# A four-layer graph network on one core: the attention's weighted sums formed with the exponentials as stationary operand

## The chip, the cores and the metric

The kernel runs on one core of a Trainium2 chip. The metric is the device time of one execution in microseconds. An execution is compared by the median of several runs; one execution was also recorded by the hardware profiler.

## What is computed

A graph of 625 nodes (768 features each) and 10,000 edges passes through four residual blocks, each behind a layer norm and a ReLU. The first two blocks are relational convolutions, the last two are attention over the edges. Cut to what matters here, an attention block does, for each head with its features `h` (8 heads of 96 in one layer, then one head of 768, and in the last block 12 heads of 64):

```
e = leaky_relu(al_s[src] + al_d[dst], 0.2)
m = segment_max(e, dst)
ex = exp(e - m[dst])
z = segment_sum(ex, dst)
out = segment_sum(h[src] * (ex / z[dst])[:, :, None], dst)
```

## The kernel before

The kernel is written engine by engine, with semaphores between them; the order of the work on each engine is the order of its program. The attention is computed densely. The edges stand as a matrix of counts between source and destination nodes, 640 x 640 with padding (`NG` = 5 tiles of `P` = 128 source nodes, `NP` = 640 destination nodes along the free axis), and its logarithm is added to the scores, so that an exponential carries the number of edges with it and is zero where there are none. What the texts below call n=0 is the layer with eight heads (`C2` = 96), n=1 the one with one head, n=2 the one with twelve (`C3` = 64). `tiles_` exists on PE and on ScalarE (ACT in the profile), `all_heads` on VectorE (DVE).

A step is one head and one tile of source nodes; there are 5 x 8 = 40 of them in n=0 and 5 x 12 = 60 in n=2, numbered k. For step k, four things happen:

- TensorE (PE) forms the *terms* in PSUM (`log_terms`, L2049): the logarithms of the counts, in a high and a low fp32r part, and the maxima per destination, as three products in two halves of 320 columns. The terms alternate between banks 0, 1 and 4, 5.
- ScalarE forms `z`, the leaky score (L829); VectorE adds the terms to it (`logits`, L1496).
- ScalarE takes the exponential into one of two buffers `pt` (L837), an array of 128 source nodes by 640 destination nodes in fp32.
- PE sums over the source nodes (L2084). Stationary is `R`, the node features of this head with a column of ones (c + 1 = 97 or 65 columns), moving is `pt`, 640 columns in two halves, in banks 2 and 3. After five steps there stand c + 1 rows of sums over 640 nodes.

PE's program is two steps ahead: the terms of k + 2 come before the sums of k. After a head's five steps, its sums stand with features along the partitions, while the output wants nodes there. So ScalarE copies them to `oT` (`sums_copy`, L845), PE transposes them in five pieces into bank 6 (`turned`, L2072), and VectorE divides by the column of ones and adds the result in (`head_out`, L1506, with L1559 for n=0 and `residual`, L1647 to L1651, for n=2). PE waits for the copy at the next head's first sums, since the banks are the same ones, and does the transposes right behind these.

VectorE also computes the next pair of heads' maxima (`maximum`, L1471), whose columns PE turns into rows (`head_rows`, L2036) and ScalarE copies (L818). In VectorE's program `head_out` of a head stands behind the fourth logits of the next one. In the last pair of heads no maximum is left. In n=0 a long pass of VectorE over the first half of the output (`elu_parts(0)`, L1549 to L1552) stands ahead of the last head's output.

A fp32 matmul appears in the trace as two records, each with its own load of the stationary operand (PEld); a transpose or a fp32r or fp16 matmul as one.

Of the kernel before, what the change touches and what calls it, by code (L numbers as in the profile page):

```python
# [21 lines left out]
P = 128  # L22
N, D, E = 625, 768, 10000
NG = -(-N // P)
NP = NG * P
# [29 lines left out]
def gnn_kernel(nc, a, out):  # L55
    ctx = ExitStack()
    with ctx:
# [19 lines left out]
        R = sb("R", [P, NG, 780])  # L77
# [5 lines left out]
        arena = sb("arena", [P, 6528 + GB * D])  # L83
# [6 lines left out]
        zt = arena[:, 2560:5760].rearrange("p (b n) -> p b n", b=NG)  # L90
        pt = arena[:, 5760:7040].rearrange("p (b n) -> p b n", b=2)
        alT = arena[0:2 * H3, 7680:8320]
        oT = arena[:, 7680:8320]
        rowD = arena[:, 8320:9600].rearrange("p (b n) -> p b n", b=2)
        mx_scr = [arena[:, o:o + NP] for o in (7040, 9600, 10240)]

# [84 lines left out]
        with nc.sbuf_tensor("sc_lo", [P, SCW], F32R) as sc_lo:  # L181
# [17 lines left out]
        ident = sb("ident", [P, P])  # L199
        iota = sb("iota", [P, P + 2])  # L200
        iota16 = sb("iota16", [P, NP + 1], F16)
        z16 = sb("z16", [P, 512], F16)
# [22 lines left out]
        ps = ctx.enter_context(nc.psum_tensor("ps", [P, 8, 512], F32))  # L225
# [25 lines left out]


        A = [{m: sem(f"{m}_{n}") for m in ("al_ok row_tp row_cp row_st rs0 rd0 mx mx_ok cl_ok c_ok z_ok l_ok p_ok o_mm o_ev"
                                           + (" rs1 rd1 o_cp o_tp o_r" if n != 1 else "")).split()} for n in range(3)]

        FT_BANK = (4, 0)
        HEADS = ((H2, C2), (1, D), (H3, C3))
# [343 lines left out]
        def _(act):  # L601
            cp, rl = ACT.Copy, ACT.Relu
# [217 lines left out]
            def tiles_(n, out_tile):  # L820
                H, s = HEADS[n][0], A[n]

                def z(it, i):

                    j, t = i // NG, i % NG
                    if t == 0:
                        act.wait_ge(s[f"rd{j % 2}"], 16 * (it + j // 2) + 16)
                    act.wait_ge(s["p_ok"], 10 * it + i + 6)
                    act.activation(zt[:, t, :], rowD[:, j % 2, :], rl,  # L829
                                   bias=AL[n][:, t, 3, ds(2 * it + j, 1)], scale=0.8).then_inc(s["z_ok"], 1)  # L830

                def e(it, i):

                    act.wait_ge(s["l_ok"], 10 * it + i + 1)
                    if H > 1:
                        act.wait_ge(s["o_mm"], 10 * it + i + 1)
                    act.activation(out_tile(i % 2, i % NG), zt[:, i % NG, :], ACT.Exp,  # L837
                                   bias=AL[n][:, i % NG, 2, ds(2 * it + i // NG, 1)]).then_inc(s["p_ok"], 1)

                def sums_copy(hd):  # L840

                    c = HEADS[n][1]
                    act.wait_ge(s["o_mm"], 5 * hd + 7)
                    act.wait_ge(s["o_tp"], hd + 1)
                    act.activation(oT[0:c + 1, :].rearrange("p (b n) -> p b n", b=2), ps[0:c + 1, 2:4, 0:NP // 2], cp).then_inc(s["o_cp"], 1)  # L845

                def heads(it, m, last):

                    for i in range(m):
                        if not (last and i + 3 >= m):  # L850
                            z(it, i + 3)
                        e(it, i)
                        first = isinstance(it, int) and it == 0
                        if H > 1 and i % NG == 0 and not (first and i == 0):
                            sums_copy(2 * it + i // NG - 1)
                        if i % NG == 4 and not last:
                            head_rows(n, it + 1, i // NG, 0)
                        if H > 1 and i == 2 and not first:
                            head_rows(n, it, 1, 1)
                        if i == NG + 2 and not last:  # L860
                            head_rows(n, it + 1, 0, 1)
                for i in range(3):
                    z(0, i)
                if H == 1:
                    heads(0, NG, True)
                else:
                    heads(0, 2 * NG, False)
                    with act.Fori(1, H // 2 - 1) as it:
                        heads(it, 2 * NG, False)
                    heads(H // 2 - 1, 2 * NG, True)  # L870
                    sums_copy(H - 1)

            act.wait_ge(S["ct_ln"], 1)
            logs(0)
# [6 lines left out]
            for k in range(2):  # L881
                act.wait_ge(S["elu_m"], k + 1)
                c = slice(k * HALF, (k + 1) * HALF)
# [35 lines left out]
        def _(dve):  # L919
# [466 lines left out]
            for k in range(2):  # L1386
                for g in range(NG):
# [7 lines left out]
                    else:  # L1395
                        ins = dve.tensor_tensor(x[:, g, :], x[:, g, :], vec[:, 1, :], ALU.add)
# [4 lines left out]
            for i in range(2 * NG):  # L1401
                c, j = i // NG, i % NG
# [95 lines left out]
            def head_out(n, it, j, put, steps):  # L1498

                H, c = HEADS[n]  # L1500
                s = A[n]
                hd = 2 * it + j
                base = steps * hd
                o = ps[:, 6, 0:NG * (c + 1)].rearrange("p (g c) -> p g c", c=c + 1)
                dve.wait_ge(s["o_tp"], hd + 2)
                dve.tensor_scalar(rz[:, j, :].unsqueeze(2), o[:, :, c:c + 1], 1e-16, None, ALU.add if n == 0 else ALU.max).then_inc(s["o_r"], 1)  # L1506
                dve.wait_ge(s["o_r"], base + 1)
                dve.reciprocal(rz[:, j, :], rz[:, j, :]).then_inc(s["o_r"], 1)
                dve.wait_ge(s["o_r"], base + 2)
                put(hd, o[:, :, 0:c], rz[:, j, :].unsqueeze(2).to_broadcast([P, NG, c]), s, base)  # L1510
# [64 lines left out]
            first = n_chain[0]  # L1575
            for i in range(4 * NG):
                c, g, k = i // (2 * NG), i // 2 % NG, i % 2
# [13 lines left out]
            for k, slope in ((2, 0.2), (3, 0.8)):  # L1591
                ins = dve.tensor_scalar(AL[1][:, :, k, :], AL[1][:, :, 0, :], slope, None, ALU.mult)
# [23 lines left out]
            for g in range(NG):  # L1616
                b = 4 + 2 * (g % 2)
# [6 lines left out]
                for k in range(2):  # L1624
                    cols = slice(k * HALF, (k + 1) * HALF)
                    ins = dve.scalar_tensor_tensor(x[:, g, cols], ps[:, b + k, 0:HALF], rz[:, 0, g:g + 1], x[:, g, cols], ALU.mult, ALU.add)
# [11 lines left out]
            for k, slope in ((2, 0.2), (3, 0.8)):  # L1638
                ins = dve.tensor_scalar(AL[2][:, :, k, :], AL[2][:, :, 0, :], slope, None, ALU.mult)
# [18 lines left out]
        def _(pe):  # L1658
# [340 lines left out]
            for i in range(2 * NG):  # L1999
                c, j = i // NG, i % NG  # L2000
# [4 lines left out]
                n = 0  # L2005
                for s in range(NG):
                    if i == 0:
                        pe.wait_ge(S["ct_lo"], s + 1)
                    for l, r in ((cg_hi, rg_hi), (cg_hi, rg_lo), (cg_lo, rg_hi)):
                        ins = pe.matmul(ps[:, 2 + i % GA, 0:HALF], l[:, s, P * j:P * (j + 1)], r[:, s, c * HALF:(c + 1) * HALF],  # L2010
                                        start=(n == 0), stop=(n == 3 * NG - 1))
# [47 lines left out]
            def tiles_(n):  # L2059

                H, c = HEADS[n]
                s = A[n]
                for m, v in (("o_mm", 2), ("o_tp", 1), ("o_ev", 2)):
                    pe.sem_inc(s[m], v)
                first_terms(n)

                def turned(hd):

                    pe.wait_ge(s["o_cp"], hd + 1)
                    pe.wait_ge(s["o_ev"], hd + 2)  # L2070
                    for g in range(NG):
                        ins = pe.transpose(ps[:, 6, (c + 1) * g:(c + 1) * (g + 1)], oT[0:c + 1, P * g:P * (g + 1)], ident[0:c + 1, 0:c + 1])  # L2072
                    ins.then_inc(s["o_tp"], 1)

                for hd in range(H):
                    for t in range(NG):
                        k = NG * hd + t
                        if k + 2 < NG * H:
                            log_terms(n, (k + 2) // (2 * NG), (k + 2) % (2 * NG))
                        if t == 0 and hd:  # L2080
                            pe.wait_ge(s["o_cp"], hd)
                        pe.wait_ge(s["p_ok"], k + 11)
                        for b in range(2):
                            ins = pe.matmul(ps[0:c + 1, 2 + b, 0:NP // 2], R[:, t, (c + 1) * hd:(c + 1) * (hd + 1)],  # L2084
                                            pt[:, k % 2, NP // 2 * b:NP // 2 * (b + 1)], start=(t == 0), stop=(t == NG - 1), skip_group_check=True)
                        ins.then_inc(s["o_mm"], 1)
                        if t == 0 and hd:
                            turned(hd - 1)
                        if t == 1 and hd and hd + 1 < H:
                            head_rows(n, hd + 1, 1)  # L2090
                        if t == 2 and hd + 2 < H:
                            head_rows(n, hd + 2, 0)
                turned(H - 1)

            for n in range(3):
                pe.sem_inc(A[n]["p_ok"], 10)
# [12 lines left out]
            for k, bank in ((0, 6), (1, 2)):  # L2109
                for b in range(2):  # L2110
                    ins = pe.matmul(ps[:, bank + b, 0:CW], ident[0:2, k:k + 1].to_broadcast([2, P]), alT[0:2, CW * b:CW * (b + 1)],
                                    start=True, stop=True)
# [7 lines left out]
            for g in range(NG):  # L2120
                b = 4 + 2 * (g % 2)
                if g >= 2:
                    pe.wait_ge(A[1]["o_ev"], g - 1)
                for k, (c0, c1) in enumerate(((0, HALF), (HALF, D + 1))):
                    for t in range(NG):
                        ins = pe.matmul(ps[:, b + k, 0:c1 - c0], h[:, t, P * g:P * (g + 1)], R[:, t, c0:c1],  # L2126
                                        start=(t == 0), stop=(t == NG - 1))
# [26 lines left out]
            for g in range(NG):  # L2154
# [5 lines left out]
                for kt in range(KT):  # L2160
                    o = 512 * FT_BANK[g % 2] + 2 * P * kt
# [28 lines left out]
```

## Time and profile before

| | before |
|---|---|
| median of 3 runs | 2178.45 us |
| lowest, highest | 2177.02, 2182.46 us |
| profiled execution | 2181.19 us, of which the span 2179.4 |
| PE busy | 1939.9 us (89%) |
| PE weight loads busy | 1699.0 us (78%) |
| DVE busy | 1211.6 us (56%) |
| ACT busy | 838.8 us (38%) |
| L2084, PE, the sums | 400 records, 125.1 us |
| mean granted clock of PE | 0.954 |

The profile is of one execution. The span is what the engines' records cover; the execution's own time is 1.8 us longer. Busy time counts overlapping records once, but a matmul's record includes the time in which it drains while the next one already streams, so a busy PE need not be at its peak. The chain of waits follows the work that ended last back through whatever released it. A weight load (PEld) can run beside a matmul.

### The profile page before, as it was taken

How to read it: one execution, taken by the hardware profiler on the slowest of the kernel's cores; microseconds unless marked ns; L12 is line 12 of the kernel's file. 1: busy time of each engine (PE TensorE's matmuls, PEld its weight loads, DVE VectorE, ACT ScalarE, POOL GpSimd, SP SyncE). 2: the span in 40 equal slices, each digit the busy share in tenths (PEclk: the TensorE clock that was granted, in tenths of full speed). 3: DMA queues.
4: the chain of work that ended last, by engine and by line, in shares of the span. 5: the costliest groups of instructions: out<-in, count | busy, mean ns of one | idle time of the engine just before them, and what ended most of it. 6: DMA issues, size and time to landing. Idle time of an engine off the chain costs nothing.

```text
span 2179.4 us, 34673 instructions
## 1 busy us (share of the span) xinstructions
PE 1939.9 (89%) x11166; PEld 1699.0 (78%) x11167; DVE 1211.6 (56%) x2275; ACT 838.8 (38%) x1125; POOL 559.0 (26%) x538
## 2 busy tenths in 40 slices
PE   5998998989999999779999999996788869878898
PEld 5887986759999977579999999996446857675676
DVE  7842223454443645565555655554555687756696
ACT  2221222332222223224555555553333128631676
POOL 0003765630000056434333444100772000000000
PEclk9999999999999999989999999998899989989999
DMA  5445667754556567657788887875883012100211
GB/s 163 151 154 167 178 170 259 267 163 127 168 168 196 172 232 246 197 175 236 263 274 267 276 265 253 285 236 184 266 271 126 8 37 61 66 15 8 68 61 54
DMA packets 203766, 377.74 MB, mean 173 GB/s; under 512 B 18937, under 2 KB 174378, under 8 KB 203670
## 3 DMA queue, kind: packets, MB, share of 16 engines
q1 hardware_dynamic: 171014, 245.57, 34.9%
q0 software_dynamic: 31216, 128.89, 18.7%
q10 hardware_dynamic: 1440, 1.97, 0.2%
q8 instruction: 65, 1.06, 0.2%
q14 instruction: 31, 0.25, 0.0%
HBM read 288.03 MB, written 88.33 MB: 173 GB/s over the span
## 4 chain that ended last, share of the span: by engine, by line
PE 38%; DVE 6%; issue 5%; DMA 4%; ACT 3%; another core or an unknown queue 1%; POOL 1%; ACTq 0%; SPq 0%; DVEq 0%; POOLq 0%
PE ps L1867 20%; PE ps L2084 4%; PE ps L2049 3%; DMA arena<-in_L_gnn_W_rel 3%; PE ps L1749 2%; PE ps L1896 2%; PE ps L2126 1%; PE ps L1744 1%; PE ps L2010 1%; PE ps L1669 1%; DMA arena<-U,ix 1%; DVE arena L1471 1%; POOL arena L529 1%; PE ps L2036 1%
## 5 line engine op out<-in xcount | busy, mean ns | idle before, releaser
L1867 PE MATMUL ps<-w_hi,hT_hi 128*128 128x384 f32 x2052 | 719.5, 351 | 45.8 <-ACT arena L615 13.8
L1867 PE MATMUL ps<-w_hi,hT_lo 128*128 128x384 f32 x2052 | 695.0, 339 | 0.3 <-issue 0.3
L1867 PE MATMUL ps<-w_lo,hT_hi 128*128 128x384 f32 x2052 | 694.9, 339 | 0.0
L1867 PEld LDWEIGHTS ps<-w_hi,hT_hi 128*128 128x128 f32 x2052 | 391.8, 191 | 55.8 <-issue 19.3
L1867 PEld LDWEIGHTS ps<-w_lo,hT_hi 128*128 128x128 f32 x2052 | 391.5, 191 | 0.4 <-issue 0.2
L529 POOL DMA_INDIRECT arena<-U,ix x252 | 272.1, 1080 | 465.4 <-DMA U<-arena 348.6
L1867 PEld LDWEIGHTS ps<-w_hi,hT_lo 128*128 128x128 f32 x2052 | 391.3, 191 | 0.0
L615 ACT ACTIVATE arena<-ps 128x384 f32<-128x384 f32 x160 | 78.2, 492 | 448.4 <-PE ps L1867 386.4
L1749 PE MATMUL ps<-arena,onehot 128*128 128x512 f32 x504 | 197.6, 516 | 20.1 <-DVE onehot_r L1087 7.5
L1749 PEld LDWEIGHTS ps<-arena,onehot 128*128 128x128 f32 x504 | 91.0, 199 | 99.9 <-issue 95.8
L565 POOL DMA_INDIRECT h<-h_d,lidx x68 | 91.5, 1346 | 295.6 <-PE ps L1896 252.0
L961 DVE TENSOR_TENSOR w_lo<-arena,w_hi 128x2304 fp32r<-128x2304 f32 x45 | 114.9, 2554 | 84.6 <-ACT w_hi L608 76.5
L738 ACT ACTIVATE msg<-arena,wgt 128x768 fp32r<-128x768 f32 x84 | 78.7, 937 | 195.6 <-DMA arena<-U,ix 162.5
L1204 DVE TENSOR_TENSOR w_lo<-arena,w_hi 128x1152 fp32r<-128x1152 f32 x67 | 91.1, 1360 | 86.4 <-ACT w_hi L675 76.7
L685 ACT ACTIVATE arena<-ps 128x384 f32<-128x384 f32 x136 | 66.2, 487 | 177.9 <-PE ps L1867 128.3
L1148 DVE SCALAR_TENSOR_TENSOR hT_lo<-ps,hT_hi 128x512 fp32r<-128x512 f32 x102 | 70.2, 688 | 110.4 <-ACT hT_hi L645 96.9
L2084 PE MATMUL ps<-arena,R 128*65 128x320 f32 (+1 forms) x400 | 125.1, 436 | 2.1 <-ACT arena L837 1.7
L1090 DVE TENSOR_SCALAR onehot<-iota,tab,wgt 128x128 f32<-128x128 f32 x126 | 46.8, 371 | 120.7 <-PE ps L1749 92.0
L1496 DVE TENSOR_TENSOR arena<-arena,ps 128x640 f32<-128x640 f32 x105 | 85.1, 819 | 43.1 <-PE ps L2049 37.2
L1080 DVE SCALAR_TENSOR_TENSOR msg<-arena,wgt,msg 128x768 fp32r<-128x768 f32 x84 | 85.2, 1014 | 40.2 <-issue 24.4
L1031 DVE TENSOR_SCALAR oh_d<-iota,tab 128x128 f16<-128x128 f16 x168 | 44.3, 264 | 100.7 <-PE ps L1711 92.4
L608 ACT ACTIVATE w_hi<-arena 128x2304 fp32r<-128x2304 f32 x45 | 95.6, 2125 | 10.1 <-issue 7.2
(289 smaller groups left out, 2920.6 us busy)
## 6 DMA issues: line engine op xcount, KB each, us to landing
arena<-in_L_gnn_W_rel SPq DMA_DIRECT2D x74, 1152.0 KB, 6.2
U<-arena SPq DMA_DIRECT2D x292, 192.0 KB
arena<-in_L_gnn_W SPq DMA_DIRECT2D x36, 1152.0 KB
U<-z SPq DMA_DIRECT2D x28, 864.0 KB
arena<-rows_d SPq DMA_DIRECT2D x40, 320.0 KB, 3.4
arena<-in_L_gnn_root SPq DMA_DIRECT2D x4, 1152.0 KB
arena<-U,ix POOLq DMA_INDIRECT x252
arena<-in_L_gnn_W_root SPq DMA_DIRECT2D x2, 1152.0 KB
```

The costliest lines, as they stand in the source:

```text
L529: pool.indirect_dma_start(out=ring[:, b, :], out_offset=None, in_=U[0:NP * (R0, R0, R1)[phase], :], in_offset=bass.IndirectOffsetOnAxis(ap ...
L565: pool.indirect_dma_start(out=src_rows[:, TC * j + g, :], out_offset=None, in_=h_d, in_offset=bass.IndirectOffsetOnAxis(ap=lidx[:, 2 * TC ...
L608: act.activation(w_hi[:, o % 2], raw[:, o % 2], cp).then_inc(S["w_hi"], 1)
L615: act.activation(dst, ps[:, (o + g) % 2, 0:HALF] if len(dst.shape) == 2 else ps[:, (o + g) % 2, 0:HALF].rearrange("p (h c) -> p h c", h=ds ...
L738: act.activation(parts_of(ph)[0][:, t // TW % MB, :], ring[:, n % RB, :], cp, scale=wgt[:, ph // 2, t:t + 1]).then_inc(S["msg_hi"], 1)
L961: dve.tensor_tensor(w_lo[:, o % 2], raw[:, o % 2], w_hi[:, o % 2].bitcast(F32), ALU.subtract).then_inc(S["w_lo"], 1)
L1080: dve.scalar_tensor_tensor(lo[:, b, :], ring[:, (NT * ph + t) % RB, :], wgt[:, ph // 2, t:t + 1], hi[:, b, :].bitcast(F32), ALU.mult, ALU. ...
L1204: dve.tensor_tensor(w_lo[:, 1 - j, 0:KT // 2], raw[:, 1 - j, 0:KT // 2], w_hi[:, 1 - j, 0:KT // 2].bitcast(F32), ALU.subtract)
L1496: dve.tensor_tensor(z, z, terms(i % 2), ALU.add).then_inc(s["l_ok"], 1)
L1749: ins = pe.matmul(sums(c0, g), onehot[:, b, :], ring[:, n % RB, c0:c1], start=False, stop=True, skip_group_check=True)
L1867: ins = pe.matmul(acc, l, r[:, j, kt, :], start=(n == 0), stop=(n == 3 * KT - 1))
L2084: ins = pe.matmul(ps[0:c + 1, 2 + b, 0:NP // 2], R[:, t, (c + 1) * hd:(c + 1) * (hd + 1)], pt[:, k % 2, NP // 2 * b:NP // 2 * (b + 1)], st ...
```

## The change

The two operands of the sums change places. Stationary is now a piece of the exponentials, 128 source nodes by 128 destination nodes; moving is `R`, with its 97 or 65 columns. Five matmuls per step take the place of two, and the result comes out with the nodes along the partitions, in one bank: five groups of c + 1 columns, 485 or 325 in all. The banks 2 and 3 alternate between heads. Since five groups share a bank, a matmul with zeros opens the bank for each head, and the sums are all added to it. ScalarE's copy, `oT`, PE's transposes and the semaphores of both are gone; VectorE reads the bank of the sums once the last of the head's sums is counted on `o_mm`. PE waits on `o_ev` for the output of the head before last in place of the copy. n=1 is untouched.

```diff
-                def sums_copy(hd):
-
-                    c = HEADS[n][1]
-                    act.wait_ge(s["o_mm"], 5 * hd + 7)
-                    act.wait_ge(s["o_tp"], hd + 1)
-                    act.activation(oT[0:c + 1, :].rearrange("p (b n) -> p b n", b=2), ps[0:c + 1, 2:4, 0:NP // 2], cp).then_inc(s["o_cp"], 1)
...
-                        if H > 1 and i % NG == 0 and not (first and i == 0):
-                            sums_copy(2 * it + i // NG - 1)
...
-                    sums_copy(H - 1)
...
-                o = ps[:, 6, 0:NG * (c + 1)].rearrange("p (g c) -> p g c", c=c + 1)
-                dve.wait_ge(s["o_tp"], hd + 2)
+                o = ps[:, 2 + j, 0:NG * (c + 1)].rearrange("p (g c) -> p g c", c=c + 1)
+                dve.wait_ge(s["o_mm"], NG * hd + NG + 2)
...
-                def turned(hd):
-
-                    pe.wait_ge(s["o_cp"], hd + 1)
-                    pe.wait_ge(s["o_ev"], hd + 2)
-                    for g in range(NG):
-                        ins = pe.transpose(ps[:, 6, (c + 1) * g:(c + 1) * (g + 1)], oT[0:c + 1, P * g:P * (g + 1)], ident[0:c + 1, 0:c + 1])
-                    ins.then_inc(s["o_tp"], 1)
...
-                        if t == 0 and hd:
-                            pe.wait_ge(s["o_cp"], hd)
+                        if t == 0 and hd >= 2:
+                            pe.wait_ge(s["o_ev"], hd + 1)
+                        if t == 0:
+                            pe.matmul(ps[:, 2 + hd % 2, 0:NG * (c + 1)], z16[:, 0:P], z16[:, 0:NG * (c + 1)], start=True, stop=False, skip_group_check=True)
                         pe.wait_ge(s["p_ok"], k + 11)
-                        for b in range(2):
-                            ins = pe.matmul(ps[0:c + 1, 2 + b, 0:NP // 2], R[:, t, (c + 1) * hd:(c + 1) * (hd + 1)],
-                                            pt[:, k % 2, NP // 2 * b:NP // 2 * (b + 1)], start=(t == 0), stop=(t == NG - 1), skip_group_check=True)
+                        for g in range(NG):
+                            ins = pe.matmul(ps[:, 2 + hd % 2, (c + 1) * g:(c + 1) * (g + 1)], pt[:, k % 2, P * g:P * (g + 1)],
+                                            R[:, t, (c + 1) * hd:(c + 1) * (hd + 1)], start=False, stop=(t == NG - 1), skip_group_check=True)
                         ins.then_inc(s["o_mm"], 1)
-                        if t == 0 and hd:
-                            turned(hd - 1)
...
-                turned(H - 1)
```

PE's order around the first step of n=2's last head, before (L2049 the terms, L2084 the sums, L2072 the transposes):

```order
L2049 MATMUL ps<-mrow,ones_r 128x320 x2
L2084 MATMUL ps<-arena,R 65x320 x2
L2072 MATMUL ps<-ident,arena 128x65 x5
L2049 MATMUL ps<-w_hi,ident_r 128x320 x2
L2049 MATMUL ps<-w_lo,ident_r 128x320 x2
```

and the same place in the changed kernel, whose line numbers are lower (L2038 the terms, L2064 the zeroing matmul, L2067 the sums):

```order
L2038 MATMUL ps<-mrow,ones_r 128x320 x2
L2064 MATMUL ps<-z 128x325
L2067 MATMUL ps<-R,arena 128x65 x5
L2038 MATMUL ps<-w_hi,ident_r 128x320 x2
L2038 MATMUL ps<-w_lo,ident_r 128x320 x2
```

The transposes behind the sums are gone, and one matmul of 325 columns stands ahead of them; the terms on both sides stand where they stood.

ScalarE's order at the end of n=2, before (L829 the scores, L837 the exponentials, L845 the copies):

```order
L837 ACTIVATE arena<-arena,al 128x640
L845 ACTIVATE arena<-ps 65x640
L829 ACTIVATE arena<-arena,al 128x640
L837 ACTIVATE arena<-arena,al 128x640 x4
L845 ACTIVATE arena<-ps 65x640
L57 UNCONDITIONAL_BRANCH
```

and in the changed kernel (L828 the scores, L836 the exponentials):

```order
L836 ACTIVATE arena<-arena,al 128x640
L828 ACTIVATE arena<-arena,al 128x640
L836 ACTIVATE arena<-arena,al 128x640 x4
L57 UNCONDITIONAL_BRANCH
```

The copies are gone and the rest closes up; PE and VectorE wait, behind the last exponential, for the last sums alone.

## Rows read from the trace of the kernel before

**Rows 1.** Windows: stretch, its length, each engine's busy time (instructions), PEclk, DMA share, GB/s.

```profile
1806.00:1886.00 80.00, 79.95 (x435) 61.84 (x434) 60.08 (x145) 63.44 (x94) 0.00 (x0) 1.00 0.15 42
...
2065.00:2152.00 87.00, 86.72 (x482) 62.86 (x480) 78.92 (x197) 68.72 (x104) 0.00 (x0) 1.00 0.22 70
```

**Rows 2.** Chain of waits, eight-head layer: start, length, engine, tile, line, instructions.

```profile
1827.72 1.24 PE ps L2084 x4
...
1836.70 1.08 PE ps L2084 x4
...
1837.78 0.88 PE ps L2049 x6
...
1838.66 1.23 PE ps L2084 x4
...
1839.89 0.42 PE ps L2072 x5
...
1842.29 0.11 PE ps L2036
...
1844.35 0.44 PE ps L2036 x4
```

**Rows 3.** Waits of DVE, 1834 to 1845: waiting for, in total, times, longest.

```profile
DVE arena L1496 <- PE ps L2049: 1.1, 1, 1.1
```

**Rows 4.** Timeline of ACT, twelve-head layer: start, length, instruction.

```profile
2075.95 0.68 ACT L845 ACTIVATE arena<-ps 65x640 f32<-65x640 f32 x1
...
2152.56 0.68 ACT L845 ACTIVATE arena<-ps 65x640 f32<-65x640 f32 x1
```

**Rows 5.** Waits of DVE, 2074 to 2085.

```profile
DVE arena L1496 <- DVE x L1651: 0.2, 1, 0.2
```

**Rows 6.** Waits of DVE, 2151 to 2162.

```profile
DVE arena L1496 <- PE ps L2049: 5.4, 5, 1.8
```

**Rows 7.** Chain of waits, twelve-head layer.

```profile
2087.62 1.29 PE ps L2084 x4
2088.92 0.31 PE ps L2072 x5
2089.22 0.93 PE ps L2049 x6
```

**Rows 8.** Timeline of PE's weight loads, fp32, 5 moving columns.

```profile
37.32 0.29 PEld L1781 LDWEIGHTS ps<-R 125*125 125x125 f32 x2 [2.10 <-DVE R L973]
37.53 0.30 PEld L1782 LDWEIGHTS ps<-R 125*128 125x128 f32 x2
37.75 0.19 PEld L1867 LDWEIGHTS ps<-w_hi,hT_hi 128*128 128x128 f32 x1
```

**Rows 9.** Timeline of PE's weight loads, fp32r, 128 and 256 moving columns in turn.

```profile
888.01 0.31 PEld L1724 LDWEIGHTS ps<-w_hi,hT_hi 128*128 128x128 f32 x2
...
890.09 0.19 PEld L1724 LDWEIGHTS ps<-w_hi,hT_hi 128*128 128x128 f32 x1
```

**Rows 10.** Chain and weight loads of the one-head layer's sums, fp32, 384 columns.

```profile
1967.43 32.57 PE ps L2126 x100
...
L2126 PEld LDWEIGHTS ps<-R,h x100: 186/190/190, 1967.4 to 1999.2; 128*128 128x128 f32 x100
```

**Rows 11.** Timeline of PE: eight zeroing matmuls of 512 columns.

```profile
331.84 1.90 PE L1699 MATMUL ps<-z 128*128 128x512 f16 x8 [0.58 <-ACT arena L615]
```

**Rows 12.** Timeline, end of the eight-head layer.

```profile
1890.62 0.64 PE L2072 MATMUL ps<-ident,arena 97*128 97x97 f32 x5 [0.80 <-ACT arena L845]
...
1892.27 0.16 DVE L1506 TENSOR_SCALAR rz<-ps 128x5 f32<-128x5 f32 x1
```

**Rows 13.** Chain of waits, end of the twelve-head layer.

```profile
2172.10 0.71 ACT arena L845
...
2172.85 0.54 PE ps L2072 x5
...
2173.42 0.17 DVE rz L1506
```

More of the change, by code:

```diff
@@ L92, in gnn_kernel @@
         alT = arena[0:2 * H3, 7680:8320]
-        oT = arena[:, 7680:8320]
         rowD = arena[:, 8320:9600].rearrange("p (b n) -> p b n", b=2)
@@ L253, in gnn_kernel @@
         A = [{m: sem(f"{m}_{n}") for m in ("al_ok row_tp row_cp row_st rs0 rd0 mx mx_ok cl_ok c_ok z_ok l_ok p_ok o_mm o_ev"
-                                           + (" rs1 rd1 o_cp o_tp o_r" if n != 1 else "")).split()} for n in range(3)]
+                                           + (" rs1 rd1 o_r" if n != 1 else "")).split()} for n in range(3)]
         FT_BANK = (4, 0)
@@ L2062, in tiles_ @@
                 s = A[n]
-                for m, v in (("o_mm", 2), ("o_tp", 1), ("o_ev", 2)):
-                    pe.sem_inc(s[m], v)
+                for m in ("o_mm", "o_ev"):
+                    pe.sem_inc(s[m], 2)
                 first_terms(n)
-                def turned(hd):
-                    pe.wait_ge(s["o_cp"], hd + 1)
-                    pe.wait_ge(s["o_ev"], hd + 2)
-                    for g in range(NG):
-                        ins = pe.transpose(ps[:, 6, (c + 1) * g:(c + 1) * (g + 1)], oT[0:c + 1, P * g:P * (g + 1)], ident[0:c + 1, 0:c + 1])
-                    ins.then_inc(s["o_tp"], 1)
                 for hd in range(H):
```

## The prediction

> **What bounds the kernel now.** The change touches two of the four layers only, the attention with eight heads (n=0, 1801 to 1893 us) and with twelve (n=2, 2040 to 2175). So I read, in this order: the windows, to see which engine fills these stretches; the chain of waits inside them, to see the steps that follow one another; and VectorE's waits, to see whether it or TensorE sets the pace. In the windows [rows 1] PE is busy nearly all the time in both, at a granted clock of 1.00 (its upper level, 2.4 GHz), but in n=2 VectorE is busy 79 of 87 us too, against 60 of 80 in n=0. Busy shares cannot tell which of two full engines leads. The chain can.
>
> In n=0 the chain is TensorE alone. A step is two groups: four records of L2084, the weighted sums (two fp32 matmuls, two records each), 1.08 us, and six of L2049, the terms, 0.88; together 1.96 [rows 2]. A head is five steps, 9.80, plus 0.16 for the wait on ScalarE's copy (1.24 and 1.23 where 1.08 is usual), 0.42 for the five transposes L2072, 0.11 and 0.44 for the row transposes L2036: 10.93, and the same group does return after 1838.66 - 1827.72 = 10.94. VectorE waits 1.1 us for PE in one such head [rows 3], so **n=0 is bound by TensorE**.
>
> In n=2 a head takes (2152.56 - 2075.95)/7 = 10.94 us [rows 4], and VectorE waits for nobody but itself [rows 5]: its five logits, five maxima and the head's output (three passes over 320 elements instead of one over 480) fill the head. **n=2 is bound by VectorE**, and the 0.21 us that PE loses there before the copied head (1.29 against 1.08) is mostly slack. Only in its last two heads, where no maximum is left to compute, does VectorE wait again, 5.4 us in one [rows 6].
>
> **What goes.** Of n=0: per head 0.16 of wait and 0.42 of transposes, 0.58. The part that counts ends with the last logits; seven heads are copied and turned before it, so 7 x 0.58 = 4.06. The eighth's copy and transposes are over at about 1891.3, but VectorE comes to its output at 1892.27, after the long ELU passes in front of it [rows 12]: no gain. Of n=2: the heads in the middle gain nothing while VectorE leads. In the opening one head is turned before VectorE takes over, 0.13 + 0.31 + 0.05 = 0.49, where 0.31 is the transposes and 0.05 the slower terms behind them (0.93 against 0.88) [rows 7]. In the last two heads 0.57 and 0.48. At the very end copy (0.71) and transposes (0.54) are bare: they lie between the last sum and VectorE, from 2172.08 to 2173.42 [rows 13], 1.3 without one hand-off. ScalarE loses twenty copies of 0.7 us, which nothing else waited for.
>
> **What comes.** A zeroing matmul of 485 or 325 fp16 columns per head. Eight of 512 take 1.90 us [rows 11], 0.24 each, so 0.22 and 0.15. In n=0 seven count (the first hides behind the wait for the first exponentials), 1.54; in n=2 one in the opening and two at the end, 0.45. The new wait on o_ev asks for the output of the head before last. VectorE runs that output before the logits on which PE's term matmuls of the same step already waited, so it costs nothing.
>
> **What is exchanged** decides. Instead of 4 records with 65 or 97 columns to load and 320 to stream, a step has 5 matmuls, 10 records, each with 128 columns to load and 65 or 97 to stream. The streams are short: transposes of 65 and 97 columns followed at 0.31/5 = 0.06 and 0.42/5 = 0.08 us [rows 7, 2]. So what counts is how often 128 fp32 columns can be loaded, L. Three places bear on it. Loads of this very kind behind matmuls of 5 columns follow at (37.75 - 37.32)/4 = 0.108 [rows 8], the lower end. Loads of fp32r, with 128 and 256 columns to stream in turn, follow at (890.09 - 888.01)/18 = 0.116 [rows 9]. And a load can run beside the stream ahead: with 384 fp32 columns a record takes 32.57/100 = 0.326, though its load alone lasts 0.19 [rows 10]. If it did not run beside a short stream, L would be 0.108 + 0.06 or 0.08, that is 0.17 or 0.19, the upper end. I take **0.112**, between the two rows whose streams are short: the type is that of the first, the stream lengths are those of the second. Then the ten take 1.12 where the four took 1.08: +0.04 a step. Over 38 steps of n=0 that is 1.52, over ten in n=2's opening and eight at its end 0.72.
>
> Against this overlap stands a rule. The Trainium skill (TensorE: Matmul & The Clock Gate, the mechanism in Part 3) says that a weight load overlaps a running matmul only when their row groups differ; here all are full height. By that rule the change would end at the upper end of L, the first rival below; for 384 columns the trace disagrees, 0.326 a record where a load after the stream would add 0.108 to it.
>
> **The sum.** n=0: 4.06 - 1.54 - 1.52 = 1.00. n=2: opening 0.49 - 0.15 - 0.40 = -0.06; last two heads 1.05 - 0.30 - 0.32 = 0.43; end 1.3. Together 2.7 us less. In the middle of n=2 PE's head becomes 10.92 - 0.57 + 0.15 + 5 x 0.04 = 10.70, still under VectorE's 10.94. The profiled execution took 2181.19 us; it would take 2178.5. That execution was 2.7 us above the median of 2178.45, so I forecast **2175.7**, 0.12% less. A measurement of this kernel can tell about 0.3%, 6.5 us, from no change: this is no change.
>
> With d = 10 L - 1.08 the gain is 4.94 - 56 d up to d = 0.09, and past it n=2's middle is bound by TensorE too and loses another 8 x (5 d - 0.455). It is zero at L = 0.117, a loss of 6.5 us at L = 0.124, a gain of 6.5 us at 0.105.
>
> **Rivals.** (1) *The short stream does not hide the load.* L = 0.19 in n=0 and 0.17 in n=2 (d = 0.8 and 0.6). n=0 loses 38 x 0.8 - 2.5 = 28, n=2's opening and end 18 x 0.6 - 0.8 = 10, its middle 8 x (3.0 - 0.455) = 20, less 1.3: about 57 us, 2235. For it: the 0.108 of rows 8 would be the same with or without overlap, since 5 columns take no time. Against it: rows 9, where a load beside 128 and 256 columns has no room for both in 0.116, and rows 10. It decides from L = 0.124 on. Chance 0.09. (2) *A smaller overhead*, L = 0.124 to 0.135, say a hand-over between load and stream that only short streams show. At 0.13 the loss is 56 x 0.22 + 8 x 0.645 - 4.9 = 12.5, 2191. For it: nothing in the trace loads ten such operands in a row with 65 or 97 columns. Chance 0.14. (3) *Loads run further ahead*, under the term streams too: a step would be the larger of all loads, 16 x 0.108 = 1.73, and all streams, 0.88 + 0.8. n=0 would gain 0.23 a step until VectorE bounds it, which is 1.1 us a head below today, so about 8; n=2 about 4 with its end: 2166. Against it: the terms' loads have 0.04 us of room each and would have to be kept in several sets, and no row shows more than one ahead. Chance 0.05; with L under 0.105, faster is 0.11. (4) *The clock falls*, because the array streams for less of each step. Streams doubled, a step would take over 1.76 + 1.1 = 2.9 us, and n=0 alone would lose 35. For it: the streams would fill two thirds of a step. Against it: nothing in today's full stretches [rows 1], which show neither. Chance 0.03.
>
> **The numbers.** The forecast (L from 0.105 to 0.124, within 6.5 us) has 0.63, faster 0.11, slower 0.09 + 0.14 + 0.03 = 0.26. The range goes from 2167, just short of rival 3, to rival 2's upper part, 2192; it leaves out rivals 1 and 4.
>
> **What would show it.** L2084's place in the chain: ten records in 1.1 to 1.16 us; over 1.24, I am wrong to the slow side. n=0's heads at 10.9 - 0.15; n=2's still 10.94 with VectorE waiting only for itself, and PE waiting for ScalarE's exponentials. The last output starts 1.3 us sooner behind the last sum. PEclk stays 1.00 in both windows. If n=2's middle heads change at all, my reading of who leads there is wrong.

## The result, and the profile after

The changed kernel takes 2171.03 us in the median of 16 runs (2165.41 to 2178.56), the kernel before 2177.1 in 16 runs beside them (2170.36 to 2185.84). The ratio is 0.9971, with a 95% interval of 0.9957 to 0.9985: a gain of 0.29%, at the edge of what a measurement can tell. Measured again, beside another set of runs of the kernel before, it was 0.9977 (0.9958 to 0.9996). I had forecast 0.12% and called it no change. The experiments further down ran on three chips, where the kernel before took 2161.8, 2159.6 and 2180.5 us in the median, so a whole time is only ever compared with the kernel before beside it; kernels for which no whole time is given ran once, and only their stretches are read.

The span of the profiled execution fell from 2179.4 to 2174.3 us, by 5.1. Not all of that belongs to the change. I cut both traces at the same events of VectorE: the first and the last logits of n=0, the first logits of n=2, and the starts of the outputs (L1506 before, L1495 after) of n=2.

| stretch, us | before | after | gain | forecast |
|---|---|---|---|---|
| n=0, first to last logits | 83.56 | 81.85 | 1.71 | 1.00 |
| n=2, first logits to second output | 28.61 | 28.60 | 0.01 | -0.06 |
| n=2, second to ninth output: seven middle heads | 76.61 | 76.61 | 0.00 | 0 |
| n=2, ninth to eleventh output | 20.44 | 19.61 | 0.83 | 0.43 |
| n=2, eleventh to twelfth output | 6.38 | 5.10 | 1.28 | 1.3 |
| sum of these | | | 3.8 | 2.7 |

The other 1.3 us of the span lie in stretches that the change does not touch (0.8 ahead of n=0's first logits, 0.5 between the two layers). Over the profiles of all kernels of this study the stretch between the two layers varied from 151.6 to 154.9 us, and n=0's first logits came between 1775 and 1811 us. So the stretches are the sharper measure here, and the table above is repeated below for each experiment.

The windows of the changed kernel, over the stretches that answer to [rows 1]:

```profile
1806.00:1883.00 77.00, 77.00 (x623) 75.73 (x622) 58.90 (x142) 58.99 (x85) 0.00 (x0) 1.00 0.18 44
...
2065.00:2149.00 84.00, 83.45 (x668) 80.62 (x666) 76.14 (x191) 63.01 (x93) 0.00 (x0) 1.00 0.21 68
```

The granted clock stayed at 1.00 in both, though TensorE now streams for less of each step. The chain of waits through one head of n=0, beside [rows 2] (L2038 the terms, L2064 the zeroing matmul, L2067 the sums, L2025 the row transposes):

```profile
1826.85 0.22 PE ps L2064
1827.07 1.09 PE ps L2067 x10
1828.15 0.90 PE ps L2038 x6
1829.06 1.09 PE ps L2067 x10
1830.15 0.11 PE ps L2025
1830.26 0.87 PE ps L2038 x6
1831.13 1.09 PE ps L2067 x10
1832.22 0.44 PE ps L2025 x4
1832.65 0.88 PE ps L2038 x6
...
1837.51 0.22 PE ps L2064
```

The four records of 1.08 us have become ten in 1.09; the wait in front of them (1.23 and 1.24) and the 0.42 of transposes are gone; 0.22 for the zeroing matmul has come. Sums and terms together, 1.09 + 0.90, are 1.99 us where they were 1.96. Where row transposes (L2025) stand between the two, the terms take 0.87 or 0.88 and the step costs nothing or 0.01 more than before. A head returns after 1837.51 - 1826.85 = 10.66 us where it was 10.94. The same in n=2, beside [rows 7]:

```profile
2094.40 0.94 PE ps L2038 x6
2095.34 0.15 PE ps L2064
2095.49 1.06 PE ps L2067 x10
2096.55 0.93 PE ps L2038 x6
```

Ten records in 1.06. And the sums' loads and matmuls as the trace groups them (min/median/max ns):

```profile
L2067 PEld LDWEIGHTS ps<-R,arena x1000: 186/192/201, 1805.5 to 2167.9; 128*128 128x128 f32 x167
...
L2067 PE MATMUL ps<-R,arena x1000: 217/275/351, 1805.5 to 2168.0; 128*128 128x65 f32 x100, 128*128 128x97 f32 x67
```

How often one load follows another is read inside a group: seven of its loads, as the timeline shows them in n=0 (97 moving columns) and in n=2 (65).

```profile
1829.12 0.86 PEld L2067 LDWEIGHTS ps<-R,arena 128*128 128x128 f32 x7
...
2152.26 0.86 PEld L2067 LDWEIGHTS ps<-R,arena 128*128 128x128 f32 x7
```

From the first start to the last end are 0.86 us, the last load itself lasts 0.19, so six intervals take 0.67: a load starts every 0.112 us, in both layers. Each lasts 192 ns from start to end, so they overlap with each other's tail and with the streams. The whole group in the chain, 1.09 and 1.06, is a little less than ten such intervals. The first of its loads has run beside the long stream of the last term; and the last of its streams is short, so that the load of the first term behind it ends in the terms' part of the chain (0.90 and 0.93 instead of 0.88). Only the sum of the two, 1.99 in both layers, is a cost.

The outputs of n=2, which cut its stretches (the second, the ninth, the eleventh and the twelfth), beside [rows 4]:

```profile
2067.00 0.16 DVE L1495 TENSOR_SCALAR rz<-ps 128x5 f32<-128x5 f32 x1
...
2143.61 0.16 DVE L1495 TENSOR_SCALAR rz<-ps 128x5 f32<-128x5 f32 x1
...
2163.22 0.16 DVE L1495 TENSOR_SCALAR rz<-ps 128x5 f32<-128x5 f32 x1
...
2168.32 0.16 DVE L1495 TENSOR_SCALAR rz<-ps 128x5 f32<-128x5 f32 x1 [2.28 <-PE ps L2067]
```

From 2067.00 to 2143.61 are seven heads of 10.94 us, as before. The end, beside [rows 13]: the chain goes from the last exponential through the last sums straight to VectorE, with no copy and no transposes between.

```profile
2166.07 0.84 ACT arena L836
...
2166.95 1.34 PE ps L2067 x10
...
2168.32 0.17 DVE rz L1495
```

### The profile page after: what moved, and what is told of

It reads as the page before. It is cut to its first block, busy times and chain, and to the rows that moved or that the text cites. A ratio compares the mean times of both kernels' runs of the same rounds, so it can differ in the third digit from the quotient of the medians.

```text
span 2174.3 us, 35621 instructions
## 1 busy us (share of the span) xinstructions
PE 1936.9 (89%) x11686; PEld 1749.4 (80%) x11687; DVE 1213.3 (56%) x2275; ACT 829.9 (38%) x1105; POOL 553.6 (25%) x538
## 4 chain that ended last, share of the span: by engine, by line
PE 39%; DVE 7%; DMA 4%; issue 4%; ACT 2%; POOL 1%; ACTq 0%; DVEq 0%; another core or an unknown queue 0%; SPq 0%; POOLq 0%
PE ps L1856 22%; PE ps L2067 3%; PE ps L2038 3%; DMA arena<-in_L_gnn_W_rel 2%; PE ps L1885 2%; PE ps L1738 2%; PE ps L2106 1%; PE ps L1999 1%; PE ps L1733 1%; PE ps L1658 1%; DMA arena<-U,ix 1%; POOL arena L528 1%; DVE arena L1460 1%; DVE arena L1485 1%; DVE h L934 0%
## 5 line engine op out<-in xcount | busy, mean ns | idle before, releaser
L1738 PE MATMUL ps<-arena,onehot 128*128 128x512 f32 x504 | 193.1, 506 | 19.8 <-DVE onehot_r L1076 7.6
L2067 PE MATMUL ps<-R,arena 128*128 128x65 f32 (+1 forms) x1000 | 124.1, 271 | 2.1 <-ACT arena L836 2.1
L2067 PEld LDWEIGHTS ps<-R,arena 128*128 128x128 f32 x1000 | 122.6, 191 | 3.4 <-ACT arena L836 2.7
```

What stands on the lines that cost most here:

```text
L1738: ins = pe.matmul(sums(c0, g), onehot[:, b, :], ring[:, n % RB, c0:c1], start=False, stop=True, skip_group_check=True)
L2067: ins = pe.matmul(ps[:, 2 + hd % 2, (c + 1) * g:(c + 1) * (g + 1)], pt[:, k % 2, P * g:P * (g + 1)], R[:, t, (c + 1) * hd:(c + 1) * (hd + ...
```

## The experiments

The stretches of the table above, for each kernel (us; n=0 first to last logits; n=2 as cut above):

| kernel | n=0 | n=2 opening | seven middle | two last | end |
|---|---|---|---|---|---|
| before | 83.56 | 28.61 | 76.61 | 20.44 | 6.38 |
| after | 81.85 | 28.60 | 76.61 | 19.61 | 5.10 |
| e_nozero | 80.46 | 28.65 | 76.61 | 19.29 | 5.10 |
| e_twozero | 83.32 | 28.75 | 76.61 | 19.88 | 5.10 |
| e_moving33 | 81.32 | 28.37 | 76.62 | 19.59 | 5.08 |
| e_load64 | 83.35 | 27.61 | 76.61 | 18.13 | 4.56 |
| e_load96 | 74.24 | 27.67 | 76.57 | 17.90 | 4.83 |
| e_dve_before | 83.60 | 28.60 | 75.68 | 20.42 | 5.97 |
| e_dve_after | 82.09 | 28.59 | 73.85 | 19.72 | 4.69 |
| e_unroll_before | 83.34 | 28.39 | 75.68 | 20.63 | 6.37 |
| e_unroll_after | 81.85 | 28.37 | 73.84 | 19.95 | 5.09 |
| e_best | 80.52 | 28.24 | 72.73 | 19.46 | 5.09 |
| e_after_again | 81.97 | 28.60 | 76.58 | 19.62 | 5.10 |
| e_best_again | 80.26 | 28.23 | 72.73 | 19.45 | 5.10 |

A stretch that an edit does not reach comes back within some 0.3 us, most within 0.1.

### Where TensorE's time counts: the zeroing matmul taken away and doubled

```diff
-                        if t == 0:
-                            pe.matmul(ps[:, 2 + hd % 2, 0:NG * (c + 1)], z16[:, 0:P], z16[:, 0:NG * (c + 1)], start=True, stop=False, skip_group_check=True)
...
-                                            R[:, t, (c + 1) * hd:(c + 1) * (hd + 1)], start=False, stop=(t == NG - 1), skip_group_check=True)
+                                            R[:, t, (c + 1) * hd:(c + 1) * (hd + 1)], start=(t == 0 and g == 0), stop=(t == NG - 1), skip_group_check=True)
```

> The changed kernel without its zeroing matmul: the first matmul of a head in its bank opens it, the four groups behind it only add. My theory (TensorE bounds the eight-head layer, VectorE the middle heads of the twelve-head layer): an eight-head head gets 0.22 us shorter (10.66 to 10.44), seven times, so 1.5 us; the middle heads of the twelve-head layer stay at 10.95; its last two heads give 0.3. Together about 1.9 us less than the changed kernel. The rival (TensorE bounds both layers) expects 0.15 us less in each of the middle heads too, together 3.1 us.

> The changed kernel with the zeroing matmul twice, so 485 or 325 more columns for each head on TensorE. My theory: an eight-head head grows by 0.20 to 0.22 us (10.66 to 10.87), the middle heads of the twelve-head layer stay at 10.95, the last two give 0.3: 1.8 us more. The rival (TensorE bounds the middle heads too) expects them at 11.09.

Taken away: n=0 fell by 1.39 us, its heads from 10.66 to 10.44, the two last heads of n=2 by 0.32, the seven middle ones by nothing. Measured whole, 0.9959 of the kernel before (0.9937 to 0.9981). Doubled: n=0 grew by 1.47, the two last by 0.27, the middle by nothing. The chain shows the second one's price in n=0 (the second is a copy of the line, right behind it):

```profile
1814.51 0.22 PE ps L2064
...
1814.73 0.21 PE ps L2065
```

So the zeroing matmul costs what I had taken, 0.22 in n=0, and n=0 is bound by TensorE while the middle of n=2 is not. The rival, TensorE bounds both, expected 11.09 in the middle; it is out. Opening the bank with the first of the sums alone, with the four other groups of columns adding behind it, does without the zeros.

### What sets the pace of the ten records: fewer moving, fewer stationary columns

```diff
-                            ins = pe.matmul(ps[:, 2 + hd % 2, (c + 1) * g:(c + 1) * (g + 1)], pt[:, k % 2, P * g:P * (g + 1)],
-                                            R[:, t, (c + 1) * hd:(c + 1) * (hd + 1)], start=False, stop=(t == NG - 1), skip_group_check=True)
+                            ins = pe.matmul(ps[:, 2 + hd % 2, (c + 1) * (g + 1) - 33:(c + 1) * (g + 1)], pt[:, k % 2, P * g:P * (g + 1)],
+                                            R[:, t, (c + 1) * (hd + 1) - 33:(c + 1) * (hd + 1)], start=False, stop=(t == NG - 1), skip_group_check=True)
```

> The changed kernel with only the last 33 of the 97 or 65 moving columns in each of the sums; it leaves out the sums of the other features. Theory A (a load of 128 fp32 columns sets the pace, the stream runs beside it): the ten records stay at 1.06 to 1.09 us in both layers, an eight-head head at 10.66. Theory B (load and stream follow one another in part, and 0.109 is made of both): the ten records lose up to 64 columns each, at 0.08 us for 97 up to 0.5 us for the ten, and an eight-head head goes towards 9.8, where VectorE bounds it.

The chain of n=0:

```profile
1817.51 1.04 PE ps L2067 x10
1818.55 0.96 PE ps L2038 x6
```

and seven loads inside a group:

```profile
1817.57 0.86 PEld L2067 LDWEIGHTS ps<-R,arena 128*128 128x128 f32 x7
```

A third of the columns, and a load still starts every 0.112 us, (0.86 - 0.19)/6. Theory B, in which load and stream follow one another, is out. The group shows 1.04 us instead of 1.09 and the terms behind it 0.96 instead of 0.90: together 2.00, as with 65 columns (1.99) and with 97 (1.99). So the terms did not become slower; the border between the two groups moved. Only where row transposes stand behind the sums, which is at two of a head's five steps, did the shorter group count: there the terms stayed at 0.87 and 0.88, and a head of n=0 went from 10.66 to 10.57.

The other operand, 64 of 128 stationary columns:

```diff
-                            ins = pe.matmul(ps[:, 2 + hd % 2, (c + 1) * g:(c + 1) * (g + 1)], pt[:, k % 2, P * g:P * (g + 1)],
+                            ins = pe.matmul(ps[0:64, 2 + hd % 2, (c + 1) * g:(c + 1) * (g + 1)], pt[:, k % 2, P * g:P * g + 64],
```

> The changed kernel with only 64 of the 128 stationary columns in each of the sums; it leaves out the sums of half of the destination nodes. Theory A (the load sets the pace): a load takes half, and then the stream of 97 columns sets it: the ten records take 0.83 to 0.88 us in the eight-head layer and 0.55 to 0.65 in the twelve-head layer. Theory C (a fixed cost per record, whatever its size, sets 0.109): they stay at 1.06 to 1.09. The eight-head head falls from 10.66 to 9.7 or so, where VectorE takes over; the middle heads of the twelve-head layer stay at 10.95 although TensorE then has over 2 us of room in each.

```profile
1817.46 0.88 PE ps L2038 x6
1818.34 0.98 PE ps L2067 x10
1819.32 1.07 PE ps L2038 x6
1820.39 0.98 PE ps L2067 x10
```

The ten records fell, but to 0.98 in n=0 (0.73 in n=2) where I expected 0.83 to 0.88 (0.55 to 0.65), and the terms behind a group grew to 1.07. (The terms ahead of the first group shown stand behind row transposes and took 0.88.) So a head of n=0 became 10.82, longer than with the full load. PE's weight loads show where it went (the last loads of the terms, the sums', the next terms'):

```profile
1813.30 0.34 PEld L2038 LDWEIGHTS ps<-mrow,ones_r 128*128 128x128 f32 x2
...
1813.82 0.86 PEld L2067 LDWEIGHTS ps<-R,arena 128*64 128x64 f32 x10 [0.19 <-issue]
...
1819.25 0.30 PEld L2038 LDWEIGHTS ps<-w_hi,ident_r 128*128 128x128 f32 x2
```

Before the first load of 64 columns the loader now waits where it did not: that load starts only after the last term's stream, not beside it. The same happens on the way back. A group starts at 1818.34 and its loads follow one another to the last; the first load of the next terms starts at 1819.25, some 0.09 us after the end of the last short stream, which began at 1819.07 and takes 0.083. Each change between 128 and 64 columns costs 0.15 to 0.17 us (0.98 against 0.83, 1.07 against 0.90), and a step has two. Inside a group the small loads do what theory A says. In n=2:

```profile
2140.61 0.37 PEld L2067 LDWEIGHTS ps<-R,arena 128*64 128x64 f32 x5
```

Four intervals in 0.37 - 0.14, so a record every 0.058 us with 65 columns to stream; in n=0, with 97, it is 0.083. In the two last heads of n=2, where the stream is short too, the gain of the small load outweighed this, 19.61 to 18.13; the middle heads did not move, although TensorE then had idle time in them. The windows of this kernel also bear on the clock:

```profile
1795.00:1865.00 70.00, 70.00 (x557) 58.67 (x556) 52.92 (x126) 54.15 (x79) 0.00 (x0) 1.00 0.17 44
```

It stayed at 1.00 in the stretch of n=0. To tell whether the exposed load comes with 64 columns or with any change of width, 96 columns:

```diff
-                            ins = pe.matmul(ps[:, 2 + hd % 2, (c + 1) * g:(c + 1) * (g + 1)], pt[:, k % 2, P * g:P * (g + 1)],
+                            ins = pe.matmul(ps[0:96, 2 + hd % 2, (c + 1) * g:(c + 1) * (g + 1)], pt[:, k % 2, P * g:P * g + 96],
```

> The changed kernel with 96 of the 128 stationary columns in each of the sums; it leaves out the sums of a quarter of the destination nodes. With 64 columns the ten records had fallen as the load, but the terms ahead of them grew from 0.90 to 1.07 us, because the first small load did not start beside the last term's stream. Theory A (the load sets the pace, with some 0.02 us on top where the stream is nearly as long): the ten records take 0.95 to 1.03 us in the eight-head layer. Theory D (the exposed first load belongs to loads of 64 columns and fewer, since the loads of 65 and 97 columns in the kernel before did not show it): the terms stay at 0.90, and an eight-head head gets shorter, to 10.2 or so. Theory E (every change of the load's width exposes it): the terms take 1.07 again and the head stays near 10.8.

```profile
1831.00 0.90 PE ps L2038 x6
1831.90 0.85 PE ps L2067 x10
...
1833.64 0.22 PE ps L2064
...
1843.12 0.22 PE ps L2064
```

The terms are back at 0.90, so theory E is out: not every change of width exposes a load. The ten records take 0.85, less than I had expected, and a head of n=0 went to 1843.12 - 1833.64 = 9.48, further than the 10.2 expected, with TensorE alone in the chain; the later heads of n=0 took 9.5 to 9.9. Theory D speaks of 64 columns and fewer, and that is not shown. The row transposes load 2 columns, and behind the sums of the changed kernel they cost 0.11 with no wait of the loader. Only behind the sums of 64 columns did they cost 0.20. What is special about 64 stays open.

In n=0 load and stream are now a tie, 0.085 a record where a stream of 97 columns alone takes 0.084 (0.42/5 in [rows 2]). Which of them sets the pace, n=2 tells, where the stream is shorter:

```profile
2156.96 0.59 PEld L2067 LDWEIGHTS ps<-R,arena 128*96 128x96 f32 x6
```

Five intervals in 0.59 - 0.17, so 0.085 again, though with 65 moving columns a record could follow every 0.058, as with the loads of 64. So it is the load, and the load goes by its columns: 0.112 for 128 and 0.085 for 96. Theory C, a fixed cost per record, is out. At the full width of 128 the load is what one waits for in both layers; it would meet the stream of 97 columns at 96 stationary columns, and that of 65 further down.

### Who leads in the middle of n=2: a pass of VectorE less, in both kernels

The addition of the residual product is left out of the output of each head of n=2.

```diff
                 dve.wait_ge(s["o_r"], base + 3)
-                dve.tensor_tensor(t, t, h[:, :, cols], ALU.add).then_inc(s["o_r"], 1)
-                dve.wait_ge(s["o_r"], base + 4)
+                dve.sem_inc(s["o_r"], 1)
```

> The kernel before with one pass less in VectorE's output of a twelve-head head: the addition of the residual product is left out. My theory (VectorE bounds the middle heads at 10.95 and TensorE follows close behind at about 10.9, including its wait for the copy): VectorE's head gets 0.6 us shorter, but a middle head only goes to 10.8 to 10.93, because TensorE takes over at once. The rival (VectorE alone bounds, TensorE has much room) expects 10.3.

> The changed kernel with the same pass left out. My theory: here TensorE's head is 10.6 us (five steps of 1.99, zeroing 0.15, row transposes 0.55), so the middle heads go from 10.95 to about 10.6 to 10.65, 0.25 less than in the kernel before with the same pass left out. That difference is the gain which the change made on TensorE and VectorE kept back, some 2 us over eight heads. The rival (the exchange gained nothing on TensorE in this layer) expects the same length as there.

A middle head took 75.68/7 = 10.81 us in the kernel before and 73.85/7 = 10.55 in the changed one. With a pass of VectorE less the change is worth 0.26 us in each middle head; with it, nothing. The gain exists on TensorE and VectorE keeps it back, and the kernel before had TensorE's head only 0.13 us shorter than VectorE's; the rivals, 10.3 for the kernel before and the same length for both, are out.

### The gain set free: VectorE's loop written out

```diff
-                with dve.Fori(1, H // 2 - 1) as it:
-                    pair(it, False, False)
+                if n == 2:
+                    for it in range(1, H // 2 - 1):
+                        pair(it, False, False)
+                else:
+                    with dve.Fori(1, H // 2 - 1) as it:
+                        pair(it, False, False)
```

> The changed kernel with VectorE's loop over the middle pairs of heads in the twelve-head layer written out, so that its waits are on constants; nothing is left out. The gaps between the three passes of the output are 0.13 us in the loop and 0.03 in the last pair, which is written out already. If these and the gap of 0.19 behind them are the loop's register arithmetic, VectorE's head gets about 0.3 us shorter and the middle heads go to 10.65, where TensorE bounds them: 8 x 0.3 = 2.4 us less. If the gaps are something else, 10.95 stays.

> The kernel before with VectorE's loop over the middle pairs of the twelve-head layer written out, nothing left out. The same edit took 0.39 us off each middle head of the changed kernel (10.94 to 10.55). My theory (TensorE, with transposes and the wait for the copy, stands at 10.8 in the kernel before): the middle heads only go to 10.8, as they did when a pass was left out. Then the change itself is worth 0.26 us a middle head wherever VectorE leaves room. The rival (the copy's wait came from VectorE's lateness and goes with it) expects under 10.7.

In the changed kernel the second pass of an output starts 0.63 us behind the first:

```profile
2089.30 0.49 DVE L1636 TENSOR_TENSOR kinv<-ps,rz 128x320 f32<-128x320 f32 x1
...
2089.93 0.49 DVE L1638 TENSOR_TENSOR kinv<-kinv,h 128x320 f32<-128x320 f32 x1
```

and with the loop written out 0.52:

```profile
2070.32 0.49 DVE L1640 TENSOR_TENSOR kinv<-ps,rz 128x320 f32<-128x320 f32 x1
...
2070.84 0.49 DVE L1642 TENSOR_TENSOR kinv<-kinv,h 128x320 f32<-128x320 f32 x1
```

A middle head went to 73.84/7 = 10.55, and its chain is TensorE's alone:

```profile
2083.25 1.06 PE ps L2071 x10
2084.31 0.93 PE ps L2042 x6
2085.25 1.06 PE ps L2071 x10
2086.31 0.93 PE ps L2042 x6
```

In the kernel before the same edit gave 75.68/7 = 10.81 and no more, so the rival's 10.7 or less is out, and VectorE then waits for PE's terms in five heads out of five:

```profile
DVE arena L1496 <- PE ps L2053: 1.7, 5, 0.3
```

Both numbers are those of the experiment with a pass left out, by another way. Measured whole, e_unroll_after took 0.9966 of the kernel before (0.9951 to 0.9982).

### Both together

e_best is the changed kernel with the two edits that leave nothing out: no zeroing matmul, and the loop written out.

> The changed kernel without the zeroing matmul and with VectorE's loop of the twelve-head layer written out, nothing left out: the eight-head layer gains 1.5 us as without the zeroing matmul alone, and the twelve-head layer 8 x 0.35 = 2.8, since TensorE's head loses 0.15 as well, and 0.3 in its last heads. Together 4.6 us less than the changed kernel, about 0.5% less than the kernel before. The rival (gains on TensorE and VectorE overlap rather than add) expects no more than the larger of both, 2.4.

> The changed kernel once more, beside the next one on the same chip: stage lengths as before (eight-head layer 81.85 us from the first to the last logits, middle seven heads of the twelve-head layer 76.61), and a time 0.15 to 0.4% below the kernel before.

> The changed kernel without its zeroing matmul and with VectorE's loop written out, once more beside it. By stages it should be 5.7 us shorter than the changed kernel (1.3 in the eight-head layer, 4.4 in the twelve-head layer), so 0.4 to 0.6% below the kernel before. If the whole time doesn't show that, the time of the other layers varies by more than the gain from one execution to the next.

By stretches e_best lies 1.3 us below the changed kernel in n=0 and 4.4 in n=2 (3.9 of it in the middle, 10.39 us a head); together 5.7, more than the 4.6 expected, and 9.6 below the kernel before. As a whole it took 0.9968 (0.9949 to 0.9987) in the first measurement and 0.9945 (0.9925 to 0.9965) in the second, where the changed kernel beside it had 0.9977. The first alone would not show it ahead of the changed kernel, and in the second the two intervals still overlap (2169.3 against 2174.1 us in the median, of 7 and 12 runs); its stretches came back within 0.3 us in both. e_best beats the kernel before in both. In the middle its chain is TensorE's alone again, and the two edits add up: the rival's 2.4 is out.

## Why the prediction was right, point by point

**Who bounds what.** That n=0 is bound by TensorE and the middle of n=2 by VectorE was right. The middle heads stayed at 10.94 to the hundredth, whatever TensorE was given or spared: with the zeroing matmul away or doubled, with a half or three quarters of the load. Only VectorE's own work moved them. Where VectorE gave way, TensorE's head showed itself as 10.81 us before, where I had 10.92, and as 10.55 after, where I had 10.70; the gain that VectorE hid is 0.26 where I had 0.22.

**What goes and what comes.** The wait for the copy, the transposes and the bare end were worth what their rows said: 1.28 at the end for 1.3. The last head of n=0 gave nothing, and the zeroing matmul cost 0.22, as taken. The new wait on o_ev cost nothing; the chain never passes through it.

**What is exchanged** had its price right and its count wrong. I took L = 0.112, between the fp32 loads of [rows 8] and the fp32r loads of [rows 9], and the loads do start every 0.112 us. The argument for it, by the length of the stream, did not hold: 97, 65 and 33 moving columns give the same. So the value was well placed between two rows, in part by luck. I then charged 0.04 at every step. The runs showed 0.03 (1.99 against 1.96) at the three steps of a head where the terms follow the sums at once, and 0.00 to 0.01 at the two with row transposes between them, 0.10 a head instead of 0.20. That is most of the way from the forecast head of n=0, 10.78, to the measured 10.66, and 0.7 us of the 1.1 that the sum missed. The sign to look for, ten records in 1.1 to 1.16, was put wrongly for the same reason: the chain gives the group 1.06 to 1.09 and the rest to the terms.

The other 0.4 are the two last heads of n=2. They were cut at their outputs, and nearly all of the miss lies in the first (10.06 to 9.43, where I had some 0.26 less): there the kernel before passes from VectorE's pace to TensorE's, and its chain goes through ScalarE's copy, 0.69 us at 2152.56. The second went from 10.38 to 10.17, about as forecast. Why the first gained more was not tested.

**The rule on overlap.** The load of 128 columns lasts 0.192 us, and the next one starts 0.112 us after it, whether 97, 65 or 33 columns stream in between; a load that waited for the stream would tell them apart. So load and stream run side by side for full-height operands too, and the rule of the Trainium skill (TensorE: Matmul & The Clock Gate, the mechanism in Part 3), that this needs different row groups, does not hold in this kernel. The overlap broke in one case, at the change between loads of 128 and of 64 stationary columns, in both directions; with 96 it did not.

**The rivals.** The short stream that does not hide the load (0.09) is out by e_moving33. The overhead that only short streams show (0.14) is out too: the interval is 0.112 with every length of stream. Loads further ahead (0.05): a step took 1.99, not 1.73, so no. The clock (0.03) stayed up, even with half the load. The measured gain, 0.29%, lies between my forecast and the bound for faster; about 0.17% of it can be traced to the change in the profiled pair, and the rest is within the interval. The medians differ by 6.1 us, and I had drawn the bound for faster at 6.5: the forecast stood by the 3.8 us of the stretches, and the whole time alone would have told little.

## What to carry to other kernels

When the operands of small fp32 matmuls change places, compare per record the longer of load and stream, from a row with the same type and the same stationary width: here 4 streams of 0.27 and 10 loads of 0.112 came out nearly equal, and the whole gain was what stood around them. Read such a price from the starts inside a group, and compare whole steps: where the chain puts the border between two groups of matmuls says little. Before counting a gain on one engine, look whether another is just as full: here 0.26 us a head stayed invisible until VectorE had less to do or its loop was written out. And where one execution differs from the next by more than the gain, cut the traces at events that both kernels have, and compare stretches.

## What the runs showed that I had not expected

- At the change from loads of 128 stationary columns to loads of 64, and back, a load did not start beside the stream ahead of it: the loader waited 0.19 us before the sums, the ten records took 0.98 us instead of the 0.83 of their inner pace, and the six terms behind them 1.07 instead of 0.90. Loads of 96 columns, those of 65 and 97 in the kernel before, and those of 2 columns of the row transposes did not show it. Halving the load made a head of n=0 slower (10.82 us against 10.66), taking a quarter off made it faster (9.48). I can state it, not explain it.
- The time of a load goes by its stationary columns, 0.112 us for 128 and 0.085 for 96 in fp32, and not at all by the stream beside it, as long as that is the shorter one.
- VectorE's loop in its loop form cost it at least 0.55 us a head of 10.94: written out, the head fell to 10.55, and without the zeroing matmul to 10.39, and in both TensorE stopped it. Whether the waits on register values, the addresses or the branch cost it, no run separates; between two passes of an output it was 0.11 us (0.63 against 0.52).
